# One transformer layer on one core: the order of score matmuls and result copies within an attention step, and the feed-forward stage written out instead of looped

## The reference, cut to what matters

```python
mod = (_silu(L0_c) @ L0_wmod).reshape(L0_c.shape[0], 6, 1, -1)
sa, ca, ga, sb, cb, gb = (mod[:, 0], ..., mod[:, 5])      # ga, gb kept away from 0
h = _layernorm(x) * (1 + ca) + sa
x = x + ga * attn(h)     # q, k rotated and normalised per head
                         # w = softmax(where(causal, qn @ kn.T / sqrt(32), min)); w @ v; @ Wo + bo
h = _layernorm(x) * (1 + cb) + sb
x = x + gb * (silu(h @ w_gate.T) * (h @ w_up.T)) @ w_down.T
```

## Time and profile before

| what | value |
|---|---|
| runs, median (lowest to highest) | 2522.72 us (2519.64 to 2523.82) |
| profiled execution, its own time | 2521.72 us |
| its span | 2519.8 us |
| mean granted clock of TensorE | 0.969 of full speed |
| busy: PE, PEld | 2316.9 us (92%), 1706.0 us (68%) |
| busy: DVE, ACT, POOL | 1170.1 (46%), 792.5 (31%), 743.2 us (29%) |
| attention's matmuls | from 405 to 1255 us |
| feed-forward's matmuls | from 1436.63 us to the end |

### The profile page before, as it was taken

How to read it: one execution, slowest core, us unless ns; L and a number is a source line. 1 busy time by engine, 2 the same in 40 slices (tenths; PEclk the granted TensorE clock), 3 DMA queues, 4 the chain that set the end, 5 groups by cost and what they waited for, 6 DMA issues and landing times. The chain is left out here.

```text
span 2519.8 us, 33443 instructions
## 1 busy us (share of the span) xinstructions
PE 2316.9 (92%) x12520; PEld 1706.0 (68%) x12520; DVE 1170.1 (46%) x1799; ACT 792.5 (31%) x1671; POOL 743.2 (29%) x823
## 2 busy tenths in 40 slices
PE   6999992899999999999858799999999999999998
PEld 4777771656655665665446587887878787878787
DVE  5999984655555555555269612212121213121212
ACT  3333331244454554454435411111111111111111
POOL 2667773011111111111167222222222222222221
PEclk8999995699999999999989899999999999999999
DMA  6122224643554365443179521212121211212111
GB/s 218 68 100 100 100 92 122 140 101 99 129 135 111 96 144 127 103 99 81 36 248 299 196 68 34 84 34 83 33 80 36 65 51 46 71 46 71 44 56 33
DMA packets 162369, 244.24 MB, mean 97 GB/s; under 512 B 17188, under 2 KB 84356, under 8 KB 161760
## 3 DMA queue, kind: packets, MB, share of 16 engines
q1 hardware_dynamic: 153760, 221.71, 30.2%
q0 software_dynamic: 7456, 18.07, 2.6%
q10 hardware_dynamic: 1056, 3.15, 0.3%
HBM read 132.74 MB, written 59.26 MB: 76 GB/s over the span
## 5 line engine op out<-in xcount | busy, mean ns | idle before, releaser
L882 DVE TENSOR_REDUCE b_top<-b_psA 128x2 f32<-128x1024 f32 (+3 forms) x384 | 363.3, 957 | 288.8 <-PE b_psA L801 165.1
L949 ACT ACTIVATE b_probT<-b_psB 128x512 f32<-128x512 f32 (+3 forms) x768 | 339.7, 491 | 348.5 <-PE b_psB L825 233.0
L1298 DVE TENSOR_TENSOR f_gu<-f_psU,f_silu 128x512 f32<-128x512 f32 x128 | 88.5, 691 | 749.3 <-PE f_psU L1359 749.3
L822 PE MATMUL b_psB<-b_stack 98*128 98x512 f32 (+3 forms) x768 | 287.5, 413 | 7.1 <-ACT b_probT L949 5.8
L801 PE MATMUL b_psA<-b_stack 96*128 96x512 f32 (+3 forms) x768 | 256.5, 392 | 27.9 <-DMA b_stack<-b_halves 20.2
L822 PEld LDWEIGHTS b_psB<-b_stack 98*128 98x128 f32 x768 | 139.8, 188 | 190.8 <-issue 118.5
L57 POOL TENSOR_TENSOR f_spots<-f_still 1x1 f32<-1x1 f32 x128 | 25.9, 202 | 794.8 <-PE f_psD L1347 788.7
L1288 ACT ACTIVATE f_silu<-f_psG 128x512 f32<-128x512 f32 x128 | 76.6, 598 | 523.5 <-PE f_psG L1359 523.5
L1345 PE MATMUL f_psD<-f_wd_hi,f_gu_hi 128*128 128x512 f32 x512 | 201.1, 393 | 22.8 <-DVE f_gu_lo L1302 12.3
L1357 PE MATMUL f_psG<-f_hT_hi,w_hi 128*128 128x512 f32 x512 | 200.6, 392 | 10.9 <-DVE f_hT_lo L1309 10.9
L1358 PE MATMUL f_psG<-f_hT_hi,w_lo 128*128 128x512 f32 x512 | 199.9, 390 | 0.0
(11 more groups left out here) (179 smaller groups left out, 4210.2 us busy)
## 6 DMA issues: line engine op xcount, KB each, us to landing
b_stack<-b_halves SPq DMA_DIRECT2D x192, 256.0 KB, 5.0
f_wd<-in_wd_t SPq DMA_DIRECT2D x128, 256.0 KB, 2.6
qkv_d<-a_t SPq DMA_DIRECT2D x32, 512.0 KB, 2.7
b_land<-qkv_d SPq DMA_DIRECT2D x32, 512.0 KB, 4.6
a_x<-in_x SPq DMA_DIRECT2D x32, 256.0 KB, 3.3
qkv_d<-a_v SPq DMA_DIRECT2D x32, 256.0 KB, 3.0
b_v<-qkv_d SPq DMA_DIRECT2D x16, 512.0 KB, 5.9
att_d<-b_att SPq DMA_DIRECT2D x16, 512.0 KB, 3.2
```

What stands on the lines that cost most here:

```text
L822: mm = pe.matmul(psB[:, i % 2, cols], stack[0:NR, n % BUFS, 0, j, kb * P:(kb + 1) * P], stack[0:NR, n % BUFS, 1, j, first * P:(half + 1) * ...
L882: dve.tensor_reduce(out, slot("score", NI * n + i)[:, :, 0:width], AX.X, ALU.max, negate=True).then_inc(s["maxed"], 1)
L949: act.activation(probT[:, (NW * n + w) % 3, j, 0:width], psB[:, i % 2, 0:width], ACT.Exp).then_inc(s["expd"], 1)
```

## The change

In attention PE does both score tiles of a step, one after the other, between the two pairs of shifts. DVE copies a finished half out (`take`) before the maxima of the step and not between them. The feed-forward stage has no hardware loop: all 128 units u = 16 i + c are written out on each engine. The split input has two buffers, and block i + 1 is split one quarter per unit in units 8 to 11 of block i. Every down product runs two units behind. The scaling of `psD` is apart from the add of the residual, has four buffers and waits for each quarter of the last down product by itself (`down_t`). The residual is loaded into the landing buffer `land`, in unit 12. POOL's dummy instruction before each split (`pause`) is gone.

```diff
@@ attention_stage, PE
-                    if score_at(k):
+                    if i == 0 and score_at(k):
                         n, w = score_at(k)
-                        score(n, 2 * w + i)
+                        score(n, 2 * w)
+                        score(n, 2 * w + 1)
@@ attention_stage, DVE
             for k in STEPS:
+                if take_at(k):
+                    take(*take_at(k))
                 for i in range(2):
                     if score_at(k):
                         n, w = score_at(k)
                         peak(n, 2 * w + i)
-                    if i == 0 and take_at(k):
-                        take(*take_at(k))
@@ ffn_stage, SP
-            stagger(sp, NB, HC, [(load_h, 0), (load_wd, 8), (store, 12), (load_x1, 14)])
+            load_h(0)
+            for u in range(NU + 3):
+                i, c = u // HC, u % HC
+                if u < NU:
+                    load_wd(u)
+                if c == 2 and 1 <= i <= NB:
+                    store(i - 1)
+                if c == 4 and i < NB - 1:
+                    load_h(i + 1)
+                if c == 12 and i < NB:
+                    load_x1(i)
@@ ffn_stage, ACT
-            stagger(act, NB, HC, [(split_h, 0), (high, 1), (gated, 0)])
+                if u >= 1:
+                    high(u - 1)
+                if i < NB - 1 and 8 <= c < 8 + KC:
+                    split_h(i + 1, c - 8)
+                if u < NU:
+                    gated(u)
@@ ffn_stage, DVE
+            def scale(i, t):
+                if t == 0:
+                    dve.wait_ge(gate_in, 16 * (i // 2 + 1))
+                    at_least(dve, s["final"], 4 * i)
+                if t < 3:
+                    dve.wait_ge(s["down_t"], 3 * i + t + 1)
+                else:
+                    dve.wait_ge(s["down"], HC * (i + 1))
+                dve.tensor_tensor(scaled[:, t], psD[:, t], gate[:], ALU.mult).then_inc(s["scaled"], 1)
...
-            stagger(dve, NB, HC, [(product, 1), (split_h, 0), (low, 1), (final, 2)])
+                if 1 <= u <= NU:
+                    product(u - 1)
+                    low(u - 1)
+                if i < NB - 1 and 8 <= c < 8 + KC:
+                    split_h(i + 1, c - 8)
+                if c == 1 and 1 <= i <= NB:
                     for t in range(4):
+                        scale(i - 1, t)
+                        if i == NB:
+                            add(i - 1, t)
+                if c == 2 and 1 <= i < NB:
+                    for t in range(4):
+                        add(i - 1, t)
@@ ffn_stage, PE
-            stagger(pe, NB, HC, [(down_early, 2), (down_last, 1), (gate_up, 0)])
+            for u in range(NU + 2):
+                if u >= 2:
+                    down(u - 2)
+                if u < NU:
+                    at_least(pe, s["silu"], u - 1)
+                    matrix(u, 0)
+                    at_least(pe, s["gu"], u - 1)
+                    matrix(u, 1)
```

More of the change, by code:

```diff
@@ L1189, in ffn_stage @@
     HC = HID // P
+    NU = NB * HC
     with ExitStack() as ctx:
@@ L1269, in _ @@
-            stagger(pool, NB, HC, [(split_wd, 0)])
+            for u in range(NU):
+                at_least(pool, s["down"], u - 1)
+                pool.wait_ge(wd_in[u % 2], 16 * (u // 2 + 1))
+                pool.tensor_scalar(wd_hi[:, u % 2], wd[:, u % 2], 1.0, 1.0, ALU.mult, ALU.mult).then_inc(s["wd_hi"], 1)
+                pool.wait_ge(s["wd_hi"], u + 1)
+                pool.tensor_tensor(wd_lo[:, u % 2], wd[:, u % 2], wd_hi[:, u % 2].bitcast(F32), ALU.subtract).then_inc(s["wd_lo"], 1)
@@ L1271, in _, with split_h @@
         @block.scalar
         def _(act):
[L1273 to L1274 removed]
+            def split_h(i, k):
+                if k == 0:
                     act.wait_ge(s["h_in"], 16 * i + 16)
[L1276 to L1283 removed]
@@ new lines, in high, with gated @@
+            def high(u):
+                act.wait_ge(s["gu"], u + 1)
+                at_least(act, s["down"], u - 1)
+                act.activation(gu_hi[:, u % 2], gu[:, u % 2], ACT.Copy).then_inc(s["gu_hi"], 1)
+            def gated(u):
+                act.wait_ge(s["gate_mm"], u + 1)
+                at_least(act, s["gu"], u - 1)
+                act.activation(silu[:, u % 2], psG[:, u % 2], ACT.Silu).then_inc(s["silu"], 1)
+            for k in range(KC):
+                split_h(0, k)
@@ L1292, in _ @@
+            for u in range(NU + 1):
+                i, c = u // HC, u % HC
+                if u >= 1:
[4 more added lines that the diff above has]
+                    gated(u)
         @block.vector
         def _(dve):
-            def product(i, c):
-                dve.wait_ge(s["up_mm"], done(i, c))
-                dve.wait_ge(s["silu"], done(i, c))
-                at_least(dve, s["gu_hi"], done(i, c - 2))
-                dve.tensor_tensor(gu[:, c % 2], psU[:, c % 2], silu[:, c % 2], ALU.mult).then_inc(s["gu"], 1)
@@ L1300, in low @@
-            def low(i, c):
-                dve.wait_ge(s["gu_hi"], done(i, c))
-                dve.tensor_tensor(gu_lo[:, c % 2], gu[:, c % 2], gu_hi[:, c % 2].bitcast(F32), ALU.subtract).then_inc(s["gu_lo"], 1)
-            def split_h(i, c):
-                if c == 0:
-                    for k in range(KC):
-                        dve.wait_ge(s["h_hi"], KC * i + (k + 1))
-                        whole, hi, lo = land[:, :, k], *[x[:, k].rearrange("p (t q) -> p t q", q=P) for x in (hT_hi, hT_lo)]
-                        dve.tensor_tensor(lo, whole, hi.bitcast(F32), ALU.subtract).then_inc(s["h_lo"], 1)
@@ L1344, in down, with matrix @@
                     out_t, cols = psD[:, t], slice(t * P, (t + 1) * P)
[L1345 to L1352 removed]
+                    pe.matmul(out_t, gu_hi[:, u % 2, cols], wd_hi[:, u % 2], start=first, stop=False)
+                    pe.matmul(out_t, gu_hi[:, u % 2, cols], wd_lo[:, u % 2], start=False, stop=False)
+                    mm = pe.matmul(out_t, gu_lo[:, u % 2, cols], wd_hi[:, u % 2], start=False, stop=end)
+                    if end and t < 3:
+                        mm.then_inc(s["down_t"], 1)
+                mm.then_inc(s["down"], 1)
+            def matrix(u, m):
+                i, c = u // HC, u % HC
+                out_c = (psG, psU)[m][:, u % 2]
                 cols = slice(c * P, (c + 1) * P)
```

145 lines of the change are left out of this document (59 added, 86 removed).

## The result

The changed kernel took 2458.58 us, median of 4 runs (2456.73 to 2459.24), against 2522.09 for the kernel before on the same chip, 4 runs: a ratio of 0.9748, 95% interval 0.9731 to 0.9765, or 63.5 us less. The forecast was 2460. The profiled execution took 2456.73 us, its span 2454.6; clock 0.97 of full speed as before.

The account below looks back on a forecast made before the run. PE was taken to bound attention and feed-forward, with late matmul starts as the winnable time. 2521.7 less 32 (attention) and 30 (feed-forward) gave 2459.7, or 2460.7 from the median, stated as 2460 us; range 2448 to 2480.

Parts of the forecast that it names:

- 0.52 less 0.1: Attention, each wide step 6 to 9: 0.52 us of PE's waits for exponents won, 0.1 still lost on shift 3.
- steps 6 to 9 come 15 times: Attention's sum: net 2.1 us per group, counted for 15 groups, 32 us.
- The copy: Attention, step 7: taking `psO` first on DVE removes the late start of `weigh`, 0.2 us per group.
- the exponents bound the stage: Rival: in attention the next step's shifts 0 and 1 wait instead, attention gives nothing, 2492 us; chance 0.06.
- shift 3's waits all stayed: Rival: in attention shift 3 still waits on exponent 1, attention gives only 14 us, 2478 us; chance 0.08.
- The sign on L822: Attention: waits of L822 on `b_probT` fall from 3.5 to under 1.5 us per group if the forecast is right.
- The middle between 3.3 and 4.1: Feed-forward, gain per block edge: 3.3 us by two waits alone, 4.1 by block spacing; 3.7 taken.
- The step that named two reasons for the first wait: Feed-forward edge: PE's 1.76 us wait laid to the last down product one unit behind and splits between `product` and `low`.
- The 1.7 us of the clock: Feed-forward, first edge: 1.7 us over the others, with clock at 0.66 after PE's standstill, counted as gained.
- The weighed rule: Feed-forward edges: DVE with both inputs in SBUF and GpSimd reading SBUF exclude each other; only adds touched, counted as nothing.
- The rival in which POOL, DVE and SP hold each other up at the edges: Feed-forward: slowed adds delay stores, weight loads and POOL's split; 15 us come back, 2475 us; chance 0.06.
- a written-out list that can't be fed: Rival: feed-forward's 128 units of fresh instructions slow the kernel; at 0.6 us per unit 2527 us; chance 0.03.

Follow-up runs that it names:

- the first experiment: Changed kernel with both attention moves (PE's order, DVE's copy) undone: 2492.22 us; kernel before with only these two moves: 2486.65 us.
- experiment 2: Changed kernel with DVE's copy back between the maxima: 2468.42 us; changed kernel with PE's old attention order, copy first: 2489.84 us.
- experiment 4: Changed kernel, each block's last down product one unit behind: 2457.86 us; kernel before, high and low parts ahead of the splits: 2503.27 us.

## Why the prediction was right

**The reading** held: in both stages the time lay in the starts that come late, and the distances between starts gave their size. The two halves add up. That the total came so near, 62 us forecast and 63.5 measured, is in part luck: by the times of the first experiment attention gave 34.5 us for 32, and feed-forward 28.9 for 30. (The range is not quite its own sum either: 45 and 31 us off 2521.7 make 2446, not 2448.)

**Attention, per group.** 2.1 us were forecast, 2.14 came. Step by step (start to start, before and after): the four wide steps 6 to 9 gave 0.41, 0.47, 0.39 and 0.41, where 0.52 less 0.1 was forecast for each, and the copy's 0.2 on top in step 7; so the price of a wide step was right and step 7 fell 0.15 short. Step 10 gave 0.26 and step 11 gave 0.15, for the 0.3 of the rest; step 2 gave 0.24 and step 3 took 0.25 back: its tile A starts as the slot comes free, as forecast, and the 0.1 that was to be lost on top is not seen. So the 2.14 is met by the mechanism, and to the second digit by small misses that cancel.

**Attention, the sum.** 32 us were forecast and 34.8 came. Of the 15 distances between group starts 13 are 2.14 shorter each, but the first (53.47 to 49.99) and the last (46.51 to 43.07) gave 3.5 and 3.4. The term "steps 6 to 9 come 15 times" took these two for groups like the others; that is the 2.7 us. In the last distance the 1.3 more is step 3: no group follows, so nothing is prepared there, and the step fell from 5.17 to 4.11 us, of which 0.95 is the copy alone (experiment 2). In the first, 1.3 us lie in its first two steps, and that is the clock's, not the change's. The granted clock over 474 to 488 us, of the kernel before and of the changed kernel (us, busy by engine with instructions, clock, DMA share, GB/s):

```profile
474.00:488.00 14.00, 12.01 (x62) 9.23 (x62) 5.34 (x6) 8.60 (x13) 2.09 (x2) 0.75 0.14 38
```

```profile
474.00:488.00 14.00, 13.26 (x75) 9.93 (x78) 6.47 (x7) 9.12 (x15) 2.09 (x2) 0.79 0.24 71
```

At a clock of 0.75 in this stretch the changed kernel with the last down product one unit behind took 51.05 us, for 53.47 before; at 0.81 the kernel before with its two list entries swapped took 52.14, for 49.99. At a like clock the first distance gave 2.2 to 2.4 us. The changed kernel run again had a clock of 1.00 there and took 48.82. So 1.1 to 1.3 of the 34.8 us come from the clock that two executions happened to have.

**The copy** was sized at 0.2 us per group, which is what it gives with PE's old order (49.41 to 49.17 us per group, 2.4 us in the medians). With the new order it is worth 9.8 us, 0.6 per group. This doesn't show in the sum, since with both moves made no copy wait is left, as forecast. But the prices by themselves were wrong: without the copy, PE's new order gives 23.8 us and not some 29.

**The rivals in attention.** Had the exponents bound the stage, or had shift 3's waits all stayed, a wide step would have gained nothing or little over 0.2; it gained 0.4, with the old feed-forward stage as with the new.

**The sign on L822** (under 1.5 us per group) was met at 1.4, but 0.84 us of it is no wait for an exponent. A threshold on a releaser's name was a weak sign; the distance between steps was the good one.

**Feed-forward.** 3.7 us per edge were forecast, 3.8 came. The middle between 3.3 and 4.1 was no reading but a compromise, and the starts settle it. At an edge of the kernel before, the first product behind each wait starts 2.15 and 1.88 us after the matmul ahead of it, and the one behind that 0.34 and 0.31 later. All else follows at 0.2267, and the block holds its full 576 recorded matmuls. These four, less 0.2267 each, make the 3.8 us. The drawn idle time of 1.76 and 1.5 is too short, since it begins at the drawn end of the matmul before, 0.39 us after its start, where the next could have started after 0.2267. The spacing gave 4.1 because 0.226 was taken for 0.2267: 576 times 0.0007 is 0.4. The waits were the cause, as the swapped entries show for the first of them. The step that named two reasons for the first wait was half right: the splits ahead of the low part are the reason, the distance of one unit is none (experiment 4). At the end 2.0 us were forecast and 1.75 came: the first scaling starts when it was said to, but from there to the last add it takes 4.98 us (2446.47 to 2451.45), and before it was 4.71 (2511.97 to 2516.68).

**The 1.7 us of the clock** at the first edge were counted as gained, and at the first edge of the changed kernel, 1536 to 1540 us, the clock is 1.00. But it was no sure gain, and it is part of the 28.75 us. The same wait at the same edge left the clock at full speed in two other profiled executions, of the kernel before with the new attention and of the kernel with its loop written out. Windows of these two, in this order:

```profile
1532.00:1545.00 13.00, 11.23 (x50) 8.96 (x50) 4.36 (x7) 3.18 (x6) 4.64 (x6) 1.00 0.14 42
```

```profile
1564.00:1574.00 10.00, 8.24 (x37) 6.50 (x36) 4.36 (x6) 2.71 (x5) 4.56 (x6) 1.00 0.10 28
```

PE stands still for 1.8 us in both, at a clock of 1.00, where the kernel before had 0.66. Each of the three has this standstill at 7 edges, and the clock fell behind one of the 21. From the first to the last matmul of the stage these two took 1073.1 and 1072.8 us, and the kernel before 1074.8. The 28.9 us that feed-forward gave in the medians are the forecast without the 1.7 (26 and 2.0). A term that rests on one execution should have been entered as a part of the range.

**The weighed rule.** The adds in SBUF now lie beside POOL's splits, the scalings out of PSUM too. Groups by line over feed-forward of the changed kernel (busy, mean ns):

```profile
L1332 DVE TENSOR_TENSOR f_land<-f_land,f_scaled 128x512 f32<-128x512 f32 x32 | 30.8, 1016 | 0.4
L1327 DVE TENSOR_TENSOR f_scaled<-f_psD,f_gate 128x512 f32<-128x512 f32 x32 | 20.1, 682 | 1.4 <-PE f_psD L1365 1.4
```

The adds are slowed, to 1016 ns on the mean and 1779 at most, against 690 for one alone at the end of the program; the scalings are not, at 682, though POOL's two instructions at 1539.98 and 1540.69 lie beside the four of 1539.21. The Trainium skill (SBUF — State Buffer, Who interferes with whom) says that a DVE instruction with two inputs in SBUF contends with GpSimd's reads and one with at most one input there, outside the 2-port modes, does not; the trace agrees. It cost nothing: PE waits for none of it, and the adds have a unit of 8.2 us. The rival in which POOL, DVE and SP hold each other up at the edges falls with it, and so does the slower one, a written-out list that can't be fed: units stayed at 130.56 / 16 = 8.16 us, while the instruction queue moved more:

```profile
q8 instruction: 91, 1.49, 0.2%
```

91 packets against 64, still 0.2%.

## What to carry to other kernels

Where an engine takes its list in order, look at what stands directly before the instruction that another engine waits for: two entries that change places in two lists gave 16 us here, without the second buffer and without writing the loop out. Price moves together and not one by one: the copy was worth 2.4 us or 9.8, and `prepare` between the products 7 us slower or 4.5 faster, depending on the other move. A gain per period times the number of periods misprices the first and the last: here nothing is prepared in the last, so a wait for the copy stood open there, and the first ran in part at a lower clock. And read a loss from the distance between starts, not from drawn idle time, which was 0.2 to 0.3 us short at each wait.

## What the runs showed that was not expected

- The loop of the feed-forward stage, with its register work on every engine, costs nothing that shows in the time: 134.33 us per block written out, 134.37 looped.
- A wait bears the name of the releaser that came last in the records. 0.84 us of pause stood as "issue" in one step, as a wait on the exponents in another and as one on DVE's maxima in a third, and a wait for DVE's copy stood once as one on ACT and once as one on a DMA.
- The standstill of PE of 1.8 us at the first edge is followed by a clock of 0.66 in one of the three profiled executions that have it, and by full speed in the other two. The clock behind the first shift differs too, 0.79 and 1.00 over 474 to 488 us in two executions of the changed kernel, whose first group took 49.99 and 48.82 us.
- The steady state is not the whole stage: with `low` one step later 4.1 us came from the 70 us in which the pipeline fills (0.8 of it was given back in the first group) and 1.1 from all the groups.
